# A hybrid layer stack on one core: the second bias's products spread over eight steps, and unread products at two waits

## The chip, the cores and the metric

The kernel runs on one core of one Trainium2 chip. The metric is device time in microseconds (us) of one execution, lower is better. TensorE is the matrix engine (PE in the profile, PEld its weight loads), VectorE is DVE, ScalarE is ACT, GpSimd is POOL; SyncE (SP) issues all DMAs.

## The reference

Four blocks are applied to `x` of 1024 tokens by 256 channels in fp32, each as `x = x + block(layernorm(x))`, but for the expert block, whose own residual adds its normalized input as well:

```python
x = x + attn_a(layernorm(x))     # state space layer, 32 heads of 64, states of 128
x = x + ffn(layernorm(x))        # experts
x = x + attn_b(layernorm(x))     # state space layer, 64 heads of 8, one group of states of 128
x = x + ffn(layernorm(x))        # experts, the same weights

def ffn(x):
    aff = sigmoid(x @ wa)                      # 16 routed experts
    topk_p, topk_i = top_k(aff, 2)             # two of them for each token
    combine = one_hot(topk_i) * (topk_p / sum(topk_p)), summed over the two
    # each expert: (gelu(x @ g + gb) * (x @ w1 + b1)) @ w2 + b2
    routed = sum over e of combine[e] * expert_e(x)
    shared = sum of 2 shared experts
    return x + shared + routed
```

The last bias `b2` of all experts is, for all tokens, one product of the routing weights (16 rows, and two rows of ones for the shared experts) with the 18 rows of `b2`.

## The kernel before

The engines' programs are written out by hand, one after the other in the order in which each engine is to work; the engines are tied by semaphores alone. `Waits.wait_ge` leaves out a wait that its engine has already passed. Each block is a stage: `first_layer`, `experts(0)`, `second_layer`, `experts(1)`.

**Experts.** There are 18 experts (the two shared ones first), each for two halves of 512 tokens: 36 steps. `up(s)` (L899) makes the two up products of a step in one of two wide PSUM tiles (`wide_of(turn)`, two banks each): two calls of `product` (L682), each six matmuls of 128x512, since an fp32 factor is held as a high and a low part and three of the four part products are made for each of two blocks of channels. ScalarE takes the gelu of the first bank, GpSimd multiplies it by the token's routing weight (`bcast`, a row that a DMA spreads over the partitions), VectorE (L1842) multiplies it into the second bank, which gives the hidden values (`hid`), and splits them in two parts (L1853, L1855). `down(s)` (L917) multiplies these by the expert's down weights: four chunks of tokens by three part products, twelve matmuls of 128x256, which add up in the four upper banks (`out_cols(c)`) over all experts. On TensorE the up products of step s are followed by the down products of step s - 2. Up products need the hidden values of two turns before, since they overwrite their tile.

**Routing weights.** VectorE finds them between the first steps (`route_first`, `route_second`). TensorE turns them with one transpose (L938) into the tile of turn 4, behind `down(1)` and ahead of `down(2)`. VectorE, after it has split the hidden values of step 2, copies them out (`route_third`, L1906); SyncE stores them to `scratch_e` and loads from there the rows for the gates and `combT`, the left operand for the bias. `up(5)` (turn 6) writes the tile again and waits for that copy. GpSimd's residual addition (L2349) stands at step 8.

**Second bias.** At step `BIAS_AT` = 8, between `up(8)` and `down(6)`, TensorE makes eight fp32 products (L946), one for each chunk of 128 tokens: 18 partitions by 128 on the left, 18 by 256 on the right. Such an fp32 product is two records in the trace.

**Second layer.** The heads are done in 16 quads of four. `exponents(k)` (L992) makes four products of 128x512, each into one of the four upper banks (`open_bank` waits until the unit four places before has been read). ScalarE takes their exponentials, VectorE and GpSimd mask them (L2004, L2421). Between them stand the products that add to the states (L1007) and read them (L1015), which VectorE works off, and `inside(k)` (L1034), which adds the masked products up in a wide tile. The fourth exponent of quad 1 takes the bank that the second addition to the states had, and waits until VectorE has read that.

**Unread products.** `keep_busy(bank, n)` (L662) makes n fp32 products of `ones` by `ones`, 128x128, into the first columns of a bank; each is overwritten later and read by nobody. The kernel has 75 of them, 150 records, mostly at the layer norms.

Of the kernel before, what the change touches and what calls it, by code (L numbers as in the profile page):

```python
# [13 lines left out]
P = 128  # L14
T, D = 1024, 256
NC = T // P
# [3 lines left out]
BANK = 512  # L20

HA, PA = 32, 64
PAIRS = HA * PA // P
# [5 lines left out]
XT = WB // P  # L29
# [11 lines left out]
TILE_OF_B = [2 + 2 * i if kind == "z" else i if i < 2 else 2 * i - 1 for kind, i in SEQ_B]  # L41

GATE_AT, SQUARE_AT, ADD_AT = (9, 11, 13), (8, 11, 13), (12, 14)
N_CONST = 17

ROWS_OF_SUMS = (0, 32)
# [2 lines left out]
EXPERTS = E + SH  # L49
# [154 lines left out]
def narrow_units(n):  # L204
    return [("nar0", n), ("nar1", n), ("narT", n)]
# [94 lines left out]
def n_router(n, name):  # L300
    return len(ROUTER) * n + ROUTER.index(name) + 1
# [6 lines left out]
STEPS = [(ORDER[p], half) for p, half in PLACES]  # L308
STEP_OF = {place: s for s, place in enumerate(PLACES)}

COMB_TURN = 4
BIAS_AT = 8
# [6 lines left out]
def turn_of(s):  # L319
    return s if s < COMB_TURN else s + 1  # L320
# [15 lines left out]
def hybrid_block(nc, io):  # L336
    with ExitStack() as ctx:
# [3 lines left out]
        sem = Sems(nc, ctx, SEMS)  # L341
# [25 lines left out]
        wide = [psum[:, 2 * i * BANK:(2 * i + 2) * BANK] for i in range(2)]  # L367
# [9 lines left out]
        def lay_out(**sizes):  # L377
            at, out = 0, {}
            for name, n in sizes.items():
                out[name] = arena[:, at:at + n]  # L380
                at += n
            assert at <= ARENA, at
            return out
# [28 lines left out]
        def term_of(j, i):  # L412
# [4 lines left out]
        G_ = lay_out(w=SLOTS * (2 * KD * F + D), wa=KD * E, gb=EXPERTS, ub=EXPERTS, aff=NC * E, key=NC * E, one=NC * E,  # L417
                     comb=NC * E, c2=NC * E, m1=NC, m2=NC, km=NC, den=NC, combT=T, b2=D, gate=3 * BANK, hid=2 * BANK)
# [58 lines left out]
        def bank_of(unit):  # L477
            n = N_FILLED[unit] - 1
            at = 4 + (n if n < AGAIN else n - AGAIN) % 4
            return psum[:, at * BANK:(at + 1) * BANK]  # L480

        def wide_of(turn):
            return wide[turn % 2]


        def sync_program(sp):
# [109 lines left out]
            def second_layer():  # L596
# [14 lines left out]

                on.wait_ge(sem["bconst"], N_CONST)
                on.wait_ge(sem["down"], len(STEPS))
# [28 lines left out]
        def tensor_program(pe):  # L642
            on = Waits(pe)

            def open_bank(unit):

                n = N_FILLED[unit] - 1
                if n >= 4:
                    before = FILLED[n - 4]
                    if before in N_DVE:  # L650
                        on.wait_ge(sem["dve_done"], N_DVE[before])
                    else:
                        on.wait_ge(sem["act_done"], N_ACT[before])
                return bank_of(unit)
# [7 lines left out]
            def keep_busy(bank, n):  # L662

                on.wait_ge(sem["const"], 1)
                for _ in range(n):
                    pe.matmul(bank[:, 0:P], ones[:, :], ones[:, :], start=True, stop=True)

            def layer_norm(k, q):

                bank = open_bank(("ln", k, q))  # L670
                if k == 2:
                    on.wait_ge(sem["x_out"], (1, 2, 4, 4)[q])
                keep_busy(bank, BUSY_NORM[k][q])
                for c in (2 * q, 2 * q + 1):
                    on.wait_ge(sem["ln_v"], NC * k + c + 1)
                    on.wait_ge(sem["ident"], 16)
                    for i in range(KD):
                        at = (c % 2) * KD + i
                        m = pe.transpose(bank[:, at * P:(at + 1) * P], v[:, c, i * P:(i + 1) * P], ident[:, :])
                m.then_inc(sem["unit"], 1)  # L680

            def product(bank, t, half, k):  # L682

                on.wait_ge(sem["split"], t + 1)
                on.wait_ge(sem["dve_done"], N_DVE["ln", k, 2 * half + 1])
                for n, (q, (i, j)) in enumerate((q, p) for q in range(KD) for p in PRODUCTS):
                    m = pe.matmul(bank, split[:, t % SPLITS, i, q, :], vT[:, j, q, half * BANK:(half + 1) * BANK],  # L687
                                  start=(n == 0), stop=(n == 3 * KD - 1))
                m.then_inc(sem["proj"], 1)
# [206 lines left out]
            def experts(n):  # L896
                k, first = 2 * n + 1, TILE_E[n]

                def up(s):  # L899
                    i, half = STEPS[s]  # L900
                    p, turn = PLACES[s][0], turn_of(s)
                    if turn - 2 == COMB_TURN:
                        on.wait_ge(sem["router"], n_router(n, "combT"))
                    elif turn >= 2:
                        on.wait_ge(sem["hid"], len(STEPS) * n + turn - 2 - (turn - 2 > COMB_TURN) + 1)
                    elif n == 0:
                        on.wait_ge(sem["x_s"], 2 * turn + 2)
                    else:
                        on.wait_ge(sem["y_out"], 2 * XT)
                        on.wait_ge(sem["rms"], 1)  # L910
                    for part in range(2):
                        product(wide_of(turn)[:, part * BANK:(part + 1) * BANK], first + 2 * p + part, half, k)

                def out_cols(c):
                    return psum[:, 4 * BANK + c * D:4 * BANK + (c + 1) * D]

                def down(s):  # L917
                    p, half = PLACES[s]
                    on.wait_ge(sem["hid_lo"], len(STEPS) * n + s + 1)
                    on.wait_ge(sem["down_lo"], EXPERTS * n + p + 1)  # L920
                    on.wait_ge(sem["act_done"], N_ACT["narT", n])
                    on.wait_ge(sem["dve_done"], N_DVE["ln", k, 3])
                    for c in range(4 * half, 4 * half + 4):
                        for m_, (iw, ih) in enumerate(PRODUCTS):
                            m = pe.matmul(out_cols(c), split_hid[:, s % 2, ih, (c % 4) * P:(c % 4 + 1) * P],  # L925
                                          split_down[:, p % DOWNS, iw], start=(p == 0 and c % 2 == 0 and m_ == 0),
                                          stop=(p == EXPERTS - 1 and m_ == 2), skip_group_check=True)
                    m.then_inc(sem["down"], 1)

                head(E, k, narrow_units(n), 2 * n + 1, lambda: up(0))  # L930
                up(1)
                up(2)
                down(0)
                up(3)
                down(1)
                on.wait_ge(sem["router"], n_router(n, "comb"))
                on.wait_ge(sem["hid"], len(STEPS) * n + COMB_TURN - 1)
                pe.transpose(wide_of(COMB_TURN)[:, 0:P], G_["comb"], ident[:, :]).then_inc(sem["exp_step"], 1)  # L938
                down(COMB_TURN - 2)
                for s in range(COMB_TURN, len(STEPS)):  # L940
                    up(s)
                    if s == BIAS_AT:
                        on.wait_ge(sem["comb"], 16 * (n + 1))
                        on.wait_ge(sem["b2"], 16 * (n + 1))
                        for c in range(NC):
                            pe.matmul(out_cols(c), G_["combT"][0:EXPERTS, c * P:(c + 1) * P], G_["b2"][0:EXPERTS, :],  # L946
                                      start=False, stop=False, skip_group_check=True)
                    if s != COMB_TURN and not (n == 0 and s == len(STEPS) - 1):
                        down(s - 2)
                    if n == 0 and s == len(STEPS) - 2:  # L950
                        down(s - 1)
                down(len(STEPS) - 2)
                if n == 0:
                    layer_norm(2, 0)
                    keep_busy(wide_of(turn_of(len(STEPS) - 2)), BUSY_LAST)
                down(len(STEPS) - 1)

            def second_layer():
# [11 lines left out]
                def turned_sums(name, src):  # L970

                    bank = open_bank(name)
                    on.wait_ge(sem["bconst"], N_CONST)
                    for q in range(HB * NC // P):
# [17 lines left out]
                def exponents(k):  # L992

                    b = k % 3
                    on.wait_ge(sem[f"mv{b}"], 64 * (k // 3 + 1))
                    for j in range(4):
                        bank = open_bank(("D", 4 * k + j))
                        pe.matmul(bank, steady[:, b, j], moving[b][:, j], start=True, stop=True).then_inc(sem["unit"], 1)  # L998

# [131 lines left out]

            first_layer()
            experts(0)
            second_layer()
            experts(1)


# [979 lines left out]
        def gpsimd_program(pool):  # L2117
# [235 lines left out]
            def fixed(part):  # L2353
# [30 lines left out]
                else:  # L2384
# [3 lines left out]
                    for row in ROWS_OF_SUMS:  # L2388
                        for piece in range(2):
                            select(st3, ALU.not_equal, 1.0, -(row + 2 * piece), [[-1, 2], [0, SUB]], 1)  # L2390
                assert done[0] == (5, 11, N_CONST)[part]

# [147 lines left out]
```

## Time and profile before

| | |
|---|---|
| timed runs | 1095.44, 1095.44, 1093.54 us; median 1095.44 |
| the profiled execution's own time | 1095.1 us |
| its span, from the first to the last instruction | 1093.8 us |
| mean granted clock of TensorE | 0.983 of full speed |
| busy: TensorE, VectorE, GpSimd, ScalarE | 95%, 71%, 63%, 56% of the span |
| first expert stage | about 570 to 752 us |
| second layer | about 752 to 915 us |
| second expert stage | about 915 to 1094 us |

Times in the trace are microseconds from the span's start. A matmul's record includes the tail until its result is there, which overlaps the next one; for the pace the starts are compared. The granted clock (PEclk) is 1.00 for 2.4 GHz and 0.50 for 1.2 GHz. What stands in square brackets behind a row is how long the engine sat idle ahead of it and who ended that.

### The profile page before, as it was taken

Reading aid. Unit: us, or ns where it says so; the run is one execution under the profiler, and the core shown is the slowest. Engines: PE = TensorE matmul, PEld = TensorE weight load, DVE = VectorE, ACT = ScalarE, POOL = GpSimd, SP = SyncE. Lnnn points to the kernel's source line nnn. Section 1 sums busy time; section 2 is a strip of 40 time slices with the busy share of each in tenths; the row PEclk is TensorE's granted clock in tenths of the full one; section 3 lists DMA queues with packets and bytes.
Section 4 is the critical chain, followed back from the end, with each engine's and each line's share of the span. In section 5 each row is a group of like instructions: output and inputs, shape, how many; then the busy total and the mean of one; then the engine's idle time right before and its main releaser. Section 6 shows DMA issues by size and latency. Waiting matters only on the chain.

```text
span 1093.8 us, 23878 instructions
## 1 busy us (share of the span) xinstructions
PE 1043.8 (95%) x9902; PEld 863.2 (79%) x9902; DVE 781.0 (71%) x1186; ACT 612.7 (56%) x945; POOL 690.1 (63%) x684
## 2 busy tenths in 40 slices
PE   8899999999999999999998999998888899999998
PEld 6688888888888888888887888887653577788887
DVE  5789887888878889788867346555858765745554
ACT  5887877776867777786715223224853534322221
POOL 4977786787867788686772667644366242356553
PEclk9999999999999999999999899999999999999999
DMA  3322211211112212101020643303111120323311
GB/s 110 111 69 78 68 59 49 69 50 68 59 49 68 73 46 78 47 24 49 1 70 5 229 135 102 103 18 107 49 53 22 35 65 3 132 95 113 123 55 39
DMA packets 47217, 75.96 MB, mean 69 GB/s; under 512 B 11330, under 2 KB 34150, under 8 KB 47110
## 3 DMA queue, kind: packets, MB, share of 16 engines
q1 hardware_dynamic: 47110, 74.44, 21.3%
q8 instruction: 79, 1.29, 0.5%
q14 instruction: 28, 0.23, 0.1%
HBM read 68.13 MB, written 2.36 MB: 64 GB/s over the span
## 4 chain that ended last, share of the span: by engine, by line
PE 66%; DVE 21%; POOL 6%; ACT 3%; issue 3%; DMA 1%; DVEq 0%; SPq 0%; POOLq 0%
PE psum L687 35%; PE psum L925 9%; DVE arena L1690 7%; PE psum L659 4%; PE psum L775 4%; PE psum L767 3%; PE psum L820 3%; DVE arena L1727 2%; PE psum L1034 2%; DVE arena L1952 1%; PE psum L998 1%; PE psum L1068 1%; DVE v L1987 1%; DVE arena L1746 1%; DVE arena L1754 1%
## 5 line engine op out<-in xcount | busy, mean ns | idle before, releaser
L687 PE MATMUL psum<-vT,split 128*128 128x512 f32 x2136 | 542.3, 404 | 10.3 <-DVE arena L1690 5.5
L687 PEld LDWEIGHTS psum<-vT,split 128*128 128x128 f32 x2136 | 394.0, 191 | 100.6 <-DVE arena L1690 7.0
L1690 DVE SCALAR_TENSOR_TENSOR arena<-psum,arena 128x1023 f32<-128x1023 f32 (+2 forms) x208 | 265.7, 1277 | 76.1 <-ACT arena L1226 52.9
L2138 POOL TENSOR_TENSOR split<-arena,split 128x256 fp32r<-128x256 f32 x178 | 132.9, 759 | 63.1 <-ACT split L1151 62.8
L2345 POOL TENSOR_TENSOR arena<-arena,bcast 128x512 f32<-128x512 f32 x64 | 83.3, 1303 | 117.7 <-ACT arena L1398 101.2
L1398 ACT ACTIVATE arena<-psum,arena 128x512 f32<-128x512 f32 x72 | 49.7, 690 | 180.7 <-PE psum L687 180.6
L1226 ACT ACTIVATE arena<-psum,arena 128x512 f32<-128x512 f32 x160 | 109.3, 691 | 72.0 <-PE psum L687 71.0
L1842 DVE SCALAR_TENSOR_TENSOR arena<-psum,arena 128x512 f32<-128x512 f32 x72 | 53.9, 748 | 122.6 <-POOL arena L2345 117.6
L925 PEld LDWEIGHTS psum<-split_down,split_hid 128*128 128x128 f32 x864 | 115.8, 196 | 10.5 <-DVE split_hid L1855 3.6
L925 PE MATMUL psum<-split_down,split_hid 128*128 128x256 f32 x864 | 118.8, 289 | 2.8 <-DVE split_hid L1855 2.8
L2165 POOL TENSOR_TENSOR arena<-arena,v 128x1021 f32<-128x1021 f32 x32 | 76.4, 2388 | 43.1 <-DVE arena L1690 43.1
L1243 ACT ACTIVATE arena<-arena 128x1024 f32<-128x1024 f32 x80 | 84.3, 1059 | 31.4 <-POOL arena L2165 19.8
L659 PE MATMUL psum<-ident,arena 128*128 128x128 f32 x568 | 73.0, 274 | 8.3 <-POOL arena L2195 4.8
L659 PEld LDWEIGHTS psum<-ident,arena 128*128 128x128 f32 x568 | 64.1, 141 | 20.0 <-POOL arena L2195 8.5
L1151 ACT CAST split<-arena 128x256 fp32r<-128x256 f32 x178 | 67.2, 401 | 4.4 <-DMA arena<-in_wd 4.4
L1855 DVE TENSOR_TENSOR split_hid<-arena,split_hid 128x512 fp32r<-128x512 f32 x72 | 64.8, 900 | 2.5
L767 PEld LDWEIGHTS psum<-arena 128*128 128x128 f32 x512 | 61.2, 192 | 2.0
L767 PE MATMUL psum<-arena 128*128 128x128 f32 x512 | 62.5, 275 | 0.0
L775 PE MATMUL psum<-arena 128*64 128x64 f32 x1792 | 61.2, 223 | 0.7 <-POOL arena L2173 0.7
L775 PEld LDWEIGHTS psum<-arena 128*64 128x64 f32 x1792 | 56.3, 138 | 6.3 <-issue 5.1
L2156 POOL TENSOR_TENSOR bcast<-bcast,arena 128x1024 f32<-128x1024 f32 x32 | 60.9, 1902 | 0.0
L1853 DVE CAST split_hid<-arena 128x512 fp32r<-128x512 f32 x72 | 41.5, 576 | 17.5 <-PE psum L925 10.5
(223 smaller groups left out, 1516.3 us busy)
## 6 DMA issues: line engine op xcount, KB each, us to landing
bcast<-scratch_a SPq DMA_DIRECT2D x32, 512.0 KB, 3.7
bcast<-scratch_e SPq DMA_DIRECT2D x32, 512.0 KB, 4.2
arena<-in_w_a SPq DMA_DIRECT2D x16, 768.0 KB, 4.4
arena<-in_wg SPq DMA_DIRECT2D x36, 128.0 KB, 3.6
arena<-in_wu SPq DMA_DIRECT2D x36, 128.0 KB, 3.5
arena<-in_wd SPq DMA_DIRECT2D x36, 128.0 KB, 3.9
arena<-in_wout_a SPq DMA_DIRECT2D x8, 256.0 KB, 2.7
arena<-in_w_b SPq DMA_DIRECT2D x10, 128.0 KB, 4.9
```

Of the source, the lines that this page charges most:

```text
L659: m = pe.transpose(bank[:, i * P:(i + 1) * P], src, ident[:, :])
L687: m = pe.matmul(bank, split[:, t % SPLITS, i, q, :], vT[:, j, q, half * BANK:(half + 1) * BANK], start=(n == 0), stop=(n == 3 * KD - 1))
L767: m = pe.matmul(chunk(bank, i), chunk(cv_a[:, j % 2, 1 + g, :], c), chunk(cv_a[:, j % 2, 3 + g, :], c), start=True, stop=True)
L775: m = pe.matmul(out[half, :], lhs[:, half], rhs, start=True, stop=True)
L925: m = pe.matmul(out_cols(c), split_hid[:, s % 2, ih, (c % 4) * P:(c % 4 + 1) * P], split_down[:, p % DOWNS, iw], start=(p == 0 and c % 2 = ...
L1151: act.copy(split[:, t % SPLITS, 0], raw).then_inc(sem["hi"], 1)
L1226: act.activation(tile[:, hs], wide_of(t)[:, hs], ACT.Identity, scale=w[:, TAPS - 1:TAPS], bias=0.0).then_inc(sem["tap0"], 1)
L1243: act.activation(tile, tile, ACT.Silu).then_inc(sem["silu"], 1)
L1690: dve.scalar_tensor_tensor(out=tile[:, s:T], in0=bank[:, 0:T - s], scalar=cw_a[:, j, i, TAPS - 1 - s:TAPS - s], in1=tile[:, s:T], op0=ALU. ...
L2138: pool.tensor_tensor(split[:, t % SPLITS, 1], raw, split[:, t % SPLITS, 0].bitcast(F32), ALU.subtract).then_inc(sem["split"], 1)
L2165: pool.tensor_tensor(tile, tile, term_of(j, i)[:, far:T], ALU.add).then_inc(sem["light"], 1)
L2345: pool.tensor_tensor(gate, gate, row_buf[b][:, half * BANK:(half + 1) * BANK], ALU.mult).then_inc(sem["gated"], 1)
```

## The change

The eight bias products are no longer made together at step 8, but one a step, at steps 8 to 15, each at the same place between `up(s)` and `down(s - 2)`. At the routing weights six unread products stand ahead of the transpose and nine behind it, ahead of `down(2)`; the wait for the hidden values, which the transpose had, now stands ahead of the six. In the second layer twelve unread products stand ahead of the fourth exponent of quad 1, in the second wide tile, which nobody uses yet.

```diff
+BUSY_COMB, BUSY_QUAD = (6, 9), 12
...
                 down(1)
+                on.wait_ge(sem["hid"], len(STEPS) * n + COMB_TURN - 1)
+                keep_busy(wide_of(COMB_TURN), BUSY_COMB[0])
                 on.wait_ge(sem["router"], n_router(n, "comb"))
-                on.wait_ge(sem["hid"], len(STEPS) * n + COMB_TURN - 1)
                 pe.transpose(wide_of(COMB_TURN)[:, 0:P], G_["comb"], ident[:, :]).then_inc(sem["exp_step"], 1)
+                keep_busy(wide_of(COMB_TURN)[:, BANK:2 * BANK], BUSY_COMB[1])
                 down(COMB_TURN - 2)
                 for s in range(COMB_TURN, len(STEPS)):
                     up(s)
-                    if s == BIAS_AT:
+                    if BIAS_AT <= s < BIAS_AT + NC:
+                        c = s - BIAS_AT
                         on.wait_ge(sem["comb"], 16 * (n + 1))
                         on.wait_ge(sem["b2"], 16 * (n + 1))
-                        for c in range(NC):
-                            pe.matmul(out_cols(c), G_["combT"][0:EXPERTS, c * P:(c + 1) * P], G_["b2"][0:EXPERTS, :],
-                                      start=False, stop=False, skip_group_check=True)
+                        pe.matmul(out_cols(c), G_["combT"][0:EXPERTS, c * P:(c + 1) * P], G_["b2"][0:EXPERTS, :],
+                                  start=False, stop=False, skip_group_check=True)
...
                     for j in range(4):
+                        if (k, j) == (1, 3):
+                            on.wait_ge(sem["z"], PAIRS + XT)
+                            keep_busy(wide[1], BUSY_QUAD)
                         bank = open_bank(("D", 4 * k + j))
```

## Rows read from the trace of the kernel before

**Rows 1.** The page: its span, and the engines' busy time.

```profile
span 1093.8 us, 23878 instructions
PE 1043.8 (95%) x9902; PEld 863.2 (79%) x9902; DVE 781.0 (71%) x1186; ACT 612.7 (56%) x945; POOL 690.1 (63%) x684
```

**Rows 2.** Stretches of both expert stages: length, each engine's busy time, PEclk, DMA.

```profile
600.35:603.70 3.35, 3.35 (x13) 2.96 (x13) 1.15 (x3) 0.00 (x0) 0.00 (x0) 0.50 0.09 24
...
621.40:624.20 2.80, 2.80 (x14) 2.43 (x14) 0.75 (x1) 0.00 (x0) 2.80 (x2) 0.99 1.07 367
624.20:631.10 6.90, 6.90 (x24) 5.53 (x23) 1.63 (x5) 0.00 (x0) 2.69 (x1) 0.51 0.41 137
...
632.50:650.00 17.50, 17.50 (x102) 15.31 (x101) 8.20 (x12) 4.82 (x11) 11.85 (x16) 1.00 0.51 158
...
968.95:972.35 3.40, 3.40 (x15) 3.28 (x15) 0.41 (x1) 0.00 (x0) 1.60 (x1) 0.50 0.00 0
```

**Rows 3.** TensorE's timeline in the first expert stage: start, length, line, operands, count.

```profile
598.04 0.30 PE L938 MATMUL psum<-ident,arena 128*128 128x128 f32 x1 [0.77 <-DVE arena L1842]
599.57 2.37 PE L925 MATMUL psum<-split_down,split_hid 128*128 128x256 f32 x12 [1.23 <-DVE split_hid L1855]
...
608.23 1.60 PE L925 MATMUL psum<-split_down,split_hid 128*128 128x256 f32 x12
609.91 2.63 PEld L687 LDWEIGHTS psum<-vT,split 128*128 128x128 f32 x12 [0.29 <-DVE arena L1842]
...
621.39 4.50 PE L946 MATMUL psum<-arena 18*128 18x256 f32 x16
...
632.47 1.60 PE L925 MATMUL psum<-split_down,split_hid 128*128 128x256 f32 x12
633.91 2.96 PE L687 MATMUL psum<-vT,split 128*128 128x512 f32 x12
636.71 1.60 PE L925 MATMUL psum<-split_down,split_hid 128*128 128x256 f32 x12
```

**Rows 4.** TensorE's timeline in the second expert stage.

```profile
942.32 0.30 PE L938 MATMUL psum<-ident,arena 128*128 128x128 f32 x1 [0.78 <-DVE arena L1842]
943.85 2.00 PE L925 MATMUL psum<-split_down,split_hid 128*128 128x256 f32 x12 [1.22 <-DVE split_hid L1855]
...
952.52 1.59 PE L925 MATMUL psum<-split_down,split_hid 128*128 128x256 f32 x12
...
965.33 3.72 PE L946 MATMUL psum<-arena 18*128 18x256 f32 x16
968.97 2.93 PE L925 MATMUL psum<-split_down,split_hid 128*128 128x256 f32 x12
...
974.78 1.60 PE L925 MATMUL psum<-split_down,split_hid 128*128 128x256 f32 x12
```

**Rows 5.** The other engines' timeline at the routing weights, first expert stage.

```profile
598.83 0.69 DVE L1855 TENSOR_TENSOR split_hid<-arena,split_hid 128x512 fp32r<-128x512 f32 x1
599.43 0.28 DVE L1906 COPY arena<-psum 128x128 f32<-128x128 f32 x1
...
607.70 2.55 POOL L2345 TENSOR_TENSOR arena<-arena,bcast 128x512 f32<-128x512 f32 x2 [9.20 <-DMA bcast<-scratch_e]
```

**Rows 6.** TensorE's timeline: five unread products, ahead of the last layer norm.

```profile
915.35 1.28 PE L666 MATMUL psum<-ones 128*128 128x128 f32 x10
```

**Rows 7.** The timeline at the second quad's exponents.

```profile
813.95 2.59 DVE L2004 TENSOR_TENSOR bcast<-bcast,arena 128x512 f32<-128x512 f32 x2
...
814.09 0.50 PE L998 MATMUL psum<-split_gate,split_down 128*128 128x512 f32 x1 [1.61 <-DVE v L1990]
814.52 1.33 PE L1007 MATMUL psum<-arena 64*128 64x512 f32 x4
```

**Rows 8.** The stretch behind them, columns as in rows 2.

```profile
815.30:818.40 3.10, 3.10 (x57) 1.01 (x58) 3.07 (x3) 0.00 (x0) 3.10 (x3) 0.50 0.23 42
```

## The prediction

> **What bounds the kernel now.** I read the totals first, then the granted clock stretch by stretch, then TensorE's order of work around the three places that the change touches. The profiled execution took 1095.1 us, 1.3 us more than its span; TensorE is busy for 95% of it [rows 1]. In both expert stages it works without a pause from the first routed steps on: a step is twelve up products and twelve down products, 1.44 us from the start of the down products to that of the next up products (632.47 to 633.91) and 2.80 us for the up products (633.91 to 636.71), 4.24 us together [rows 3]. So in these stages the time is the number of columns divided by the granted clock. The reader should look at the column PEclk: it stands at 1.00 (2.4 GHz) nearly everywhere, and at 0.50 (1.2 GHz) in a few stretches. One follows the waits at the routing weights, from 600.35 to 603.70: TensorE had done one transpose between two waits of 0.77 and 1.23 us [rows 2, 3]; the second stage has its like. Others begin while the eight bias products run (624.20 to 631.10) [rows 2] or at their end (968.95 to 972.35) [rows 2]. There TensorE had been busy all the time, but with operands of 18 partitions. The change goes for these stretches and for a third kind, in the heads of the second layer (815.30 to 818.40) [rows 8].
>
> **Part 1, the bias products one a step.** None is added or removed. Eight products are sixteen records; in the second stage they take from 965.33 to 968.97, 3.64 us, so 0.455 us a product [rows 4], almost all at full clock. Then come the down products (1.44) and the up products (2.80) [rows 3]. At full clock the bundle, the down and the up behind it would last 3.64 + 1.44 + 2.80 = 7.88 us. They lasted 632.47 - 621.39 = 11.08 us in the first stage [rows 3] and 974.78 - 965.33 = 9.45 us in the second [rows 4]. The half clock cost 3.20 and 1.57 us. With one product among twenty-four full ones a step becomes 4.24 + 0.455 = 4.70 us with a tenth of it on 18 partitions. I take it that the clock stays at 2.4 GHz, as it does through the plain steps from 632.50 on [rows 2]: gain 3.20 + 1.57 = 4.77 us. The bounds: nothing regained (0) and all (4.77). The change of operand between the full and the 18-partition products, which was met once a stage, now comes eight times; no row shows its price apart, I take 0, and at most 0.1 us a product, about half of the 0.2275 us of a record [rows 4], 16 x 0.1 = 1.6 us. What the pause hid: GpSimd's long residual addition stands at the same step and is not on TensorE's path, because a step's gate is needed only two steps later.
>
> At this place the trace and a rule part. In the stretch 621.40 to 624.20 TensorE is busy for 2.80 of 2.80 us, and the clock falls right behind it [rows 2]. The Trainium skill, "TensorE: Matmul & The Clock Gate", section "What's actually happening", says that the gate follows how busy the engine has been recently. By that rule an engine that never paused should have kept its clock, the bundle would not be the cause, and spreading it would give nothing (the first rival); by the rows it is the only thing in either stage that comes just ahead of a fall without a wait.
>
> **Part 2, fifteen unread products at the routing weights, in each stage.** An unread product is two records; ten records last 1.28 us with the last one's tail of 0.27 us, so 0.112 us a record and 0.225 a product [rows 6]. Six cost 1.35 us, nine 2.02 us. The wait for the hidden values (597.9, where the transpose at 598.04 was let go [rows 3]) now comes ahead of the six, and the transpose behind them: 598.04 + 1.35 = 599.39. It ends 0.30 us later at 599.69. VectorE, who copies it, was free at 599.43 anyway, since it was at its splitting of the hidden values until then [rows 5]; so the copy comes 0.26 us later, not 1.35. Behind the copy on the path: the store of the weights, the row's load, GpSimd's gate at 607.70, which waited for that load [rows 5], VectorE's hidden values, and the up products at 609.91, which waited for those [rows 3].
> TensorE itself: nine unread products from 599.46 to 601.48, the down products to 602.92, and the two ups to 602.92 + 5.60 = 608.52 at full clock. Before, the down products began at 599.57 and the two ups ended at 608.23 [rows 3]. So the fill is paid with 1.91 us and gets the half clock back, and is 0.29 us behind. Its next down products end at 608.52 + 1.44 = 609.96, which is ahead of the released ups at 609.91 + 0.26 = 610.17. First stage: +0.26 us, set by the row's path; that the half clock is gone buys nothing there.
> Second stage: the transpose stood at 942.32, so it comes at 943.67, the nine end at 945.76, the down products at 947.20, the two ups at 952.80; before it was 952.52 [rows 4]. +0.28 us. Bounds: if no half clock is regained, the down products are late by 1.91 and 945.76 - 943.85 = 1.91 us, of which the first stage hides 0.24 us (609.91 against 608.23 + 1.44): +1.67 and +1.91. At the other end, a fill that delays nothing and regains all: 0 in the first stage, which waits for the row anyway, and -(8.67 - 7.04) = -1.63 in the second (943.85 to 952.52 against 1.44 + 5.60) [rows 4]; six and nine products between two waits that leave 1.23 us of room [rows 3] can't do that, so I stay by the sum.
>
> **Part 3, twelve unread products before the fourth exponent of the second quad.** 12 x 0.225 = 2.69 us. The fourth exponent came at 814.09 after a wait of 1.61 us [rows 7], so the third ended at 812.48, and what follows it could have begun a tail of 0.27 us earlier, at 812.2. The fourth then comes about 812.2 + 2.69 = 814.9, 0.8 us later than before. The state additions behind it come at about 815.3 in place of 814.52; they lasted 1.33 us with the clock falling under them [rows 7], and at full clock end by about 816.4. VectorE reads them after its masks, which last from 813.95 to 816.54 [rows 7]: just in time. The half clock from 815.30 to 818.40 would go, which spares TensorE up to 1.55 us, but VectorE has no gap in that stretch (3.07 of 3.10 us busy) [rows 8] and TensorE waits for it afterwards. I take 0, since it is VectorE whose row is full. Bounds: -1.55 (all of it arrives) and +0.8 (the delay arrives).
>
> **Sum.** -4.77 + 0.26 + 0.28 + 0 = -4.23 us on 1095.1: 1090.9. The three timed runs were 1095.44 twice and 1093.54, so the profiled execution is within 0.4 us of their median; forecast 1091.0.
>
> **Rivals.**
> 1. The bundle isn't what lowers the clock, and it falls in these steps as before (the rule above). Then parts 2 and 3 alone remain: 1095.1 + 0.54 = 1095.6. Against: it fell in both stages at the same instructions, and in none of the plain steps. Chance 0.05.
> 2. Slower: the unread products are work on TensorE's path and buy no clock, since the wait of 0.8 us ahead of them stays and the falls come from it. Price 1.67 + 1.91 + 0.8 = 4.4 us, at down products and exponents. It decides the sign once the bias gives back less than 4.4 us; slower by 0.2% (2.2 us) needs the bias to give less than 2.2: to 1099.5. For it: waits as short as this stand close before a fall. Against: the two waits of 0.77 and 1.23 us [rows 3] become one. Chance 0.05.
> 3. The falls don't lie the same in each execution, since one and the same bundle cost 3.20 us in one stage and 1.57 in the other. Then the bias gives back 1.57 twice: 1095.1 - 3.14 + 0.54 = 1092.5. If besides a fill of part 2 regains nothing in the second stage, because nothing had fallen there, 1.63 us more: 1094.1. For it: the timed runs lie 1.9 us apart, about one such stretch. Chance 0.20, half of it below 1093.2.
> 4. Part 3 bears fruit: the states go round faster once TensorE is at full clock, and a later fall is put off as well: 1.5 to 3 us more, 1088 to 1089.5. Against: VectorE is full there. Chance 0.15.
>
> **How the numbers follow.** Forecast 1091.0, own range 1089.7 to 1092.5, chance 0.55. A measurement tells about 0.2% from no change, here 2.2 us: faster is below 1093.2. Faster: 0.55 + 0.15 + 0.10 = 0.80. Within: 0.05 + 0.10 = 0.15. Slower: 0.05. The range goes to 1088.6 and 1093.8; it leaves out rivals 1 and 2, the upper end of 3 and the lower of 4, together under 0.2.
>
> **What the profile after would show.** Right: the unread products rise from 150 records by 2 x 30 + 24 to 234; PEclk 1.00 through steps 8 to 15 of both stages, each 4.70 us; 1.00 behind the transpose, with down products about 1.9 us later and the second up ending 0.3 us later than before; the second quad's fourth exponent about 0.8 us later and VectorE's order unmoved. Wrong: a half clock within the steps that hold a bias product (part 1), one behind the nine unread products (part 2), gaps of VectorE around 816 (part 3), or steps with a bias product longer than 4.8 us at full clock (the change of operand has a price).

## The result, and the profile after

The changed kernel takes 1102.72 us (median of nine runs, 1097.37 to 1106.06) against 1095.3 us of the kernel before (nine runs, 1093.52 to 1097.79): a ratio of 1.0064, with an interval of 1.0044 to 1.0084. The forecast was 1091.0 with a range of 1088.6 to 1093.8, faster with a chance of 0.8. It was slower, by about 7 us. The profiled execution after took 1103.7 us, its span is 1102.4 us. The page after, lines that answer to [rows 1]:

```profile
span 1102.4 us, 24043 instructions
PE 1052.5 (95%) x9986; PEld 866.3 (79%) x9986; DVE 785.1 (71%) x1186; ACT 613.1 (56%) x945; POOL 695.0 (63%) x684
```

The stretches of the expert stages after (length, each engine's busy time, PEclk, DMA), which answer to [rows 2]:

```profile
600.00:618.00 18.00, 18.00 (x108) 15.80 (x108) 9.36 (x13) 4.48 (x9) 8.10 (x8) 1.00 0.63 206
618.00:660.00 42.00, 42.00 (x219) 32.56 (x218) 23.82 (x29) 9.95 (x21) 32.63 (x35) 1.00 0.49 161
962.00:1010.00 48.00, 48.00 (x253) 37.78 (x252) 26.21 (x32) 11.55 (x25) 30.81 (x27) 1.00 0.35 114
```

All half clocks of the expert stages are gone from this execution: 1.00 behind the routing weights and through the steps with a bias product, as forecast. So the clock does what was forecast, and the kernel is slower. Where the time went is seen by comparing the starts of the same work in the two traces:

| the same place | before | after | after minus before |
|---|---|---|---|
| first down products, first expert stage | 591.43 | 591.30 | -0.13 |
| ups released by the first row | 609.91 | 609.85 | -0.06 |
| turning the narrow product, second layer | 762.17 | 761.35 | -0.82 |
| first exponent of quad 0 | 807.94 | 808.82 | +0.88 |
| the 128 small products ahead of the first `finish` | 862.27 | 860.77 | -1.50 |
| the first of the 24 products of the output | 895.07 | 900.43 | +5.36 |
| turning the narrow product, second expert stage | 929.40 | 936.56 | +7.16 |
| down products of step 3, second expert stage | 952.52 | 959.99 | +7.47 |
| last 36 down products | 1085.03 | 1093.64 | +8.61 |

The first expert stage gained 0.7 us, the second lost about 1.4, and the heads of the second layer, between 862 and 930, lost over 8 us. TensorE's timeline in the first expert stage after, which answers to [rows 3]:

```profile
597.82 1.60 PE L668 MATMUL psum<-ones 128*128 128x128 f32 x12 [0.68 <-DVE arena L1849]
599.26 0.27 PE L941 MATMUL psum<-ident,arena 128*128 128x128 f32 x1
599.37 2.17 PE L668 MATMUL psum<-ones 128*128 128x128 f32 x18
601.30 1.67 PE L927 MATMUL psum<-split_down,split_hid 128*128 128x256 f32 x12
602.80 5.76 PE L689 MATMUL psum<-vT,split 128*128 128x512 f32 x24
608.41 1.60 PE L927 MATMUL psum<-split_down,split_hid 128*128 128x256 f32 x12
609.85 2.96 PE L689 MATMUL psum<-vT,split 128*128 128x512 f32 x12
...
618.33 2.96 PE L689 MATMUL psum<-vT,split 128*128 128x512 f32 x12
621.22 0.69 PE L950 MATMUL psum<-arena 18*128 18x256 f32 x2
621.84 1.69 PE L927 MATMUL psum<-split_down,split_hid 128*128 128x256 f32 x12
623.37 2.96 PE L689 MATMUL psum<-vT,split 128*128 128x512 f32 x12
```

The fill at the routing weights went as worked out: the two ups end at 608.41, 0.31 us later than before once the start of the stage (-0.13) is taken off (forecast 0.29). But a step with one bias product lasts 623.37 - 618.33 = 5.04 us, not 4.70. Its weight loads show why (the same stretch on PEld, the engine's weight loads):

```profile
621.22 0.29 PEld L950 LDWEIGHTS psum<-arena 18*128 18x128 f32 x2 [0.36 <-issue]
621.84 1.49 PEld L927 LDWEIGHTS psum<-split_down,split_hid 128*128 128x128 f32 x12 [0.33 <-issue]
623.25 2.64 PEld L689 LDWEIGHTS psum<-vT,split 128*128 128x128 f32 x12
```

Elsewhere a load starts ahead of the product that uses it (623.25 for the ups at 623.37). At the bias product it starts together with it, and so does the load behind it: the loads stand idle for 0.36 and 0.33 us at each change of kind. The kernel before has the same two waits at its bundle, once a stage (second expert stage, PEld):

```profile
965.33 3.31 PEld L946 LDWEIGHTS psum<-arena 18*128 18x128 f32 x16 [0.36 <-issue]
968.97 2.64 PEld L925 LDWEIGHTS psum<-split_down,split_hid 128*128 128x128 f32 x12 [0.33 <-issue]
```

That one kind is plain fp32 and the other the split operands is not enough for it. The unread products are plain fp32 too, on 128 partitions, and the loads of the down products behind them start without a wait, at 601.27 against 601.30 for the first product:

```profile
601.27 1.49 PEld L927 LDWEIGHTS psum<-split_down,split_hid 128*128 128x128 f32 x12
```

What the bias products have beside that is operands of 18 partitions; no run varied that number.

In the heads the reader is to look at the waits put down to "issue", time in which TensorE waited for nothing that the profile shows. TensorE's timeline after, the three long ones:

```profile
862.18 0.66 PE L1053 MATMUL psum<-ident,arena 64*128 64x64 f32 x8
864.33 1.44 PE L1053 MATMUL psum<-ident,arena 64*128 64x64 f32 x22 [1.48 <-issue]
...
867.36 1.19 PE L1041 MATMUL psum<-v,arena 64*32 64x64 f32 x101 [0.45 <-DVE arena L2018]
871.24 0.67 PE L1041 MATMUL psum<-v,arena 64*32 64x64 f32 x27 [2.69 <-issue]
...
900.29 0.21 PE L1041 MATMUL psum<-v,arena 64*32 64x64 f32 x1 [2.53 <-issue]
900.43 7.13 PE L1075 MATMUL psum<-arena 128*128 128x256 f32 x24
```

They stand in the middle of a group of equal instructions, once with a single record of 128 left to do. In the kernel before, the thirty records of the first group (L1046 there) and the 128 of the second (L1034) go through unbroken:

```profile
863.68 2.00 PE L1046 MATMUL psum<-ident,arena 64*128 64x64 f32 x30
...
867.27 1.47 PE L1034 MATMUL psum<-v,arena 64*32 64x64 f32 x128 [0.47 <-DVE arena L2011]
```

At the second and the third of the long waits the clock falls to half (stretches as above):

```profile
871.00:877.00 6.00, 5.76 (x162) 4.38 (x162) 2.22 (x3) 2.65 (x6) 0.00 (x0) 0.50 0.12 27
897.80:900.20 2.40, 0.00 (x0) 0.00 (x0) 0.20 (x1) 0.00 (x0) 2.40 (x2) 1.00 0.03 7
901.50:905.00 3.50, 3.50 (x10) 2.81 (x9) 0.00 (x0) 0.00 (x0) 2.79 (x5) 0.55 0.02 5
```

The kernel before had such waits too, nine of them in this layer, but none above 1.29 us. I counted the matmul records from the first transpose of the tokens on (804.08 before, 804.95 after) to each such wait. Before, they stand at 584, 710, 837, 963, 1343, 1471, 1598, 1725 and 2361: 126 to 128 apart, or a multiple. With a weight load for each record that is some 254 instructions. After, they stand at 1188, 1315 and 2205. Their sum is not what differs: 7.0 us before, 6.7 after. A theory follows: TensorE's instructions arrive in blocks, a block's end comes at a fixed count of instructions, and what a stall costs depends on where in the work that end falls. Parts 2 and 3 add instructions and move it. The Trainium skill, "Runtime: NRT & Kernel Launch", section "Instruction fetch mechanics", says that an engine's instructions are refilled in blocks of 256, and that crossing a block's end is mostly hidden. The distance agrees with the trace; "mostly hidden" doesn't hold for this layer, with 7.0 us of such waits before. That these waits are waits for instructions is inferred from their even distances, not seen in the profile.

### The profile page after: what moved, and what is told of

Read it like the earlier page. It is cut to its first block, busy times and chain, and to the rows that moved or that the text cites. A ratio compares the mean times of both kernels' runs of the same rounds, so it can differ in the third digit from the quotient of the medians.

```text
span 1102.4 us, 24043 instructions
## 1 busy us (share of the span) xinstructions
PE 1052.5 (95%) x9986; PEld 866.3 (79%) x9986; DVE 785.1 (71%) x1186; ACT 613.1 (56%) x945; POOL 695.0 (63%) x684
## 3 DMA queue, kind: packets, MB, share of 16 engines
q8 instruction: 79, 1.29, 0.5%
## 4 chain that ended last, share of the span: by engine, by line
PE 66%; DVE 23%; POOL 4%; issue 3%; ACT 3%; DMA 0%; DVEq 0%; POOLq 0%
PE psum L689 35%; PE psum L927 9%; DVE arena L1697 7%; PE psum L661 4%; PE psum L777 4%; PE psum L769 4%; PE psum L822 3%; DVE arena L1734 2%; DVE v L1994 1%; DVE arena L1959 1%; DVE arena L1753 1%; DVE arena L1761 1%; PE psum L950 1%; PE psum L1041 1%; DVE v L1997 1%
## 5 line engine op out<-in xcount | busy, mean ns | idle before, releaser
L689 PEld LDWEIGHTS psum<-vT,split 128*128 128x128 f32 x2136 | 389.5, 188 | 99.4 <-DVE arena L1697 7.2
L927 PEld LDWEIGHTS psum<-split_down,split_hid 128*128 128x128 f32 x864 | 111.4, 191 | 10.7 <-issue 5.3
L1860 DVE CAST split_hid<-arena 128x512 fp32r<-128x512 f32 x72 | 46.7, 649 | 14.0 <-PE psum L927 7.9
```

## The experiments

Two theories were to be told apart: that the loss is the direct price of the added and spread products, or that it comes from the place of the instruction stream's stalls. All experiments were timed in five rounds, each row of runs beside its own runs of the kernel before.

**Part 1 alone (bias_only).** The bias products one a step, and no unread products:

```diff
+BIAS_PER, BIAS_STEPS = 1, [8, 9, 10, 11, 12, 13, 14, 15]
...
-                    if s == BIAS_AT:
+                    if s in BIAS_STEPS:
+                        at = BIAS_STEPS.index(s) * BIAS_PER
...
-                        for c in range(NC):
+                        for c in range(at, at + BIAS_PER):
```

> Only part 1: the eight bias products one a step, no unread products added. Theory (each lone bias product makes its step 0.80 us longer at full clock, since the weights of the two kinds of product don't load ahead of each other): steps 8 to 15 last 5.05 us each, 6.4 us in all against 6.84 and 5.21 us that the bundles cost before, so -0.4 us in the first stage, +1.2 us in the second, +0.8 us in all: about 1096. Rival (the loss of the changed kernel comes from the unread products alone): the gain forecast for part 1 shows, steps of 4.70 us, 1090.5.

Measured: 1096.72 against 1093.19 us, ratio 1.0028 (1.0011 to 1.0044). Slower, and by more than the +0.8 us expected. The stalls in the heads stand at the same nine counts as before (584 to 2361), as they must, since nothing was added. Its steps 8 to 15 are at PEclk 1.00:

```profile
618.00:660.00 42.00, 42.00 (x219) 32.56 (x218) 24.10 (x29) 10.26 (x23) 33.57 (x36) 1.00 0.51 173
```

So the lone products' price is real, and the clock held. That the sum is worse than +0.8 is taken up under the table.

**Part 2 alone (comb_only).** The six and nine unread products in both stages, as in the diff of the change.

> Only part 2: six and nine unread products at the routing weights of both stages. By the direct cost +0.1 us in the first and +0.3 us in the second stage: 1095.8. If the longer instruction stream in front of the second layer is what rearranges TensorE's stalls for instructions in the heads (the stalls that the profile calls issue), this kernel, which has as many instructions ahead of the heads as the changed one, shows stalls of over 2 us there, and 1099 to 1102. If the loss in the second layer comes from part 3: no such stalls, 1095.8.

Measured: 1093.89 against 1093.19 us, ratio 1.0001 (0.9984 to 1.0018). The stalls did move: one of 2.54 us at count 1315 (before: 1343) and one of 0.25, in place of nine. But their sum fell from 7.0 to 2.8 us, and the time stayed the same. So moving them can be harmless, even to one wait as long as the changed kernel's; the expectation of 1099 was wrong. The long one stands three records ahead of the end of its group:

```profile
866.17 1.44 PE L1037 MATMUL psum<-v,arena 64*32 64x64 f32 x125 [0.46 <-DVE arena L2014]
870.15 0.42 PE L1037 MATMUL psum<-v,arena 64*32 64x64 f32 x3 [2.54 <-issue]
```

**Part 3 alone (quad_only).** The twelve unread products in the second quad.

> Only part 3: twelve unread products ahead of the fourth exponent of quad 1. Theory that this is what harms the second layer: stalls of over 2 us behind quad 8 as in the changed kernel, 1099 to 1102. Theory that the instructions ahead of the second layer matter: about 1095 here, the half clock behind the exponent gone, VectorE's order unmoved.

Measured: 1092.51 against 1093.19 us, ratio 0.999 (0.9969 to 1.001). One stall of 1.56 and one of 0.24 us. No loss from it by itself that is clear of the noise.

**Waits that have passed (pad_30).** The kernel before with instructions added that do nothing:

```diff
+                    if n == 0 and 18 <= s < 28:
+                        for _ in range(3):
+                            pe.wait_ge(sem["const"], 1)
```

> The kernel before with thirty waits that have long been passed, three in each of ten steps of the first expert stage, on TensorE: no product more, only 30 instructions more, which is what fifteen unread products (a weight load and a product each) put in front of the second layer. If the place of the instructions in the stream decides the stalls in the heads: stalls rearranged as in the changed kernel, 1098 to 1101. If it doesn't: 1095.4, the same as before within 0.2%.

Measured: 1091.84 against 1093.19 us, ratio 0.9981 (0.9964 to 0.9999). The padded steps mostly last 4.24 us as ever, so the waits are free; the stalls moved by only about 7 records and stayed of the old kind (eight, of at most 1.57 us). It doesn't tell the theories apart, but it gives a tool: a way to move the stalls without a product. It is a caution as well: its interval ends just under 1 though nothing but passed waits was added, so a ratio of 0.998 by itself is no proof that an edit gains anything.

**The changed kernel again (after_again), and parts 2 and 3 together (comb_quad).**

> The changed kernel once more, beside the others of this row. Part 1 alone came to 1.0028 of before, part 2 to 1.0001, part 3 to 0.999, together 1.0019, but the changed kernel to 1.0064. If the parts add up and the difference is the spread of the executions: 1.002, 1095. If parts 2 and 3 together rearrange the stalls for instructions in the heads (3 stalls of 1.5 to 2.7 us instead of 9 of at most 1.3): 1.005 to 1.007 again, with the three stalls in the same places.

Measured: 1099.64 against 1094.89 us, ratio 1.0044 (1.0026 to 1.0061), with stalls at the same counts as in the first profile, 1188, 1315 and 2205, and one at 1442. The two measurements of the same kernel, 1.0064 and 1.0044, agree within their intervals.

> Parts 2 and 3 without part 1 (the bias products together again): if the two rearrange the stalls together, about 1.003 to 1.004 of before with three long stalls in the heads as in the changed kernel; if the parts add up: 0.999 to 1.000.

Measured: 1097.88 against 1094.89 us, ratio 1.0028 (1.0009 to 1.0048). Neither part costs anything alone that shows, and together they cost 3 us. Its timeline has the same breaks as the changed kernel's, 8 and 22 records, 101 and 27, 127 and 1, and one more of 1.55 us at 1442:

```profile
863.54 0.66 PE L1053 MATMUL psum<-ident,arena 64*128 64x64 f32 x8
865.83 2.60 PE L1053 MATMUL psum<-ident,arena 64*128 64x64 f32 x22 [1.63 <-issue]
...
870.36 1.73 PE L1041 MATMUL psum<-v,arena 64*32 64x64 f32 x101
873.62 0.44 PE L1041 MATMUL psum<-v,arena 64*32 64x64 f32 x27 [1.54 <-issue]
...
902.62 0.21 PE L1041 MATMUL psum<-v,arena 64*32 64x64 f32 x1 [1.98 <-issue]
```

**Moving the stalls there, and back (pad_230, comb_quad_pad).** The first adds 230 passed waits to the kernel before (23 in place of 3 in the diff of pad_30), the second adds 420 (21 a step in steps 14 to 33) to parts 2 and 3.

> The kernel before with 230 waits that have long been passed, 23 in each of ten steps of the first expert stage; nothing else. Thirty such waits cost no time in their steps and moved TensorE's stalls for instructions 7 matmul records ahead, so 230 should move them by 53 or 54, which is where parts 2 and 3 together put them (1343 before, 1188 and 1315 with 24 records of part 3 in the count, 127 apart). If the place of the stalls is the cause: long stalls within L1046's thirty records, within the 128 records behind them and ahead of L1068's twenty-four, and 1.002 to 1.004 of before. If it is something else in the unread products (their place at the waits, the heads' banks): 1.000.

Measured: 1098.38 against 1095.59 us, ratio 1.0022 (1.0005 to 1.004), with stalls at 1160, 1287, 1414, 2049 and 2177. The first two of them in TensorE's timeline:

```profile
861.28 0.44 PE L1049 MATMUL psum<-ident,arena 64*128 64x64 f32 x4
863.44 1.87 PE L1049 MATMUL psum<-ident,arena 64*128 64x64 f32 x26 [1.73 <-issue]
...
867.25 1.50 PE L1037 MATMUL psum<-v,arena 64*32 64x64 f32 x97
870.48 0.46 PE L1037 MATMUL psum<-v,arena 64*32 64x64 f32 x31 [1.74 <-issue]
```

No product was added, and the stalls are within four records of where parts 2 and 3 put them (the 24 records of part 3 taken off), with a loss of the same size. The page explains the quarter of a record for each wait: it counts 15 more instructions in pad_30 and 115 more in this kernel (23993 against 23878), one for each two waits. At two instructions a record that is 7.5 and 57.5 records, and the stalls moved by 7 and 56.

> Parts 2 and 3, and 420 passed waits in twenty steps of the first expert stage, which should move the stalls another 98 records, by 127 with part 2's own 29, one whole distance between two stalls, so that in the heads they stand where part 3 alone has them (one of 1.56 us). If the place of the stalls is the cause: 0.999 to 1.000 of before instead of 1.0028. If not: 1.0028 again.

Measured: 1094.15 against 1095.59 us, ratio 0.9994 (0.9974 to 1.0015): the loss of 1.0028 is gone though still more instructions were added. The page counts 210 more instructions than comb_quad's, 105 records, and the stalls moved by 104. The thirty records of L1056 (L1053 in comb_quad) go through unbroken and the block's end falls four records ahead of the end of the next group:

```profile
861.44 2.00 PE L1056 MATMUL psum<-ident,arena 64*128 64x64 f32 x30
...
865.02 1.44 PE L1044 MATMUL psum<-v,arena 64*32 64x64 f32 x124
868.48 0.30 PE L1044 MATMUL psum<-v,arena 64*32 64x64 f32 x4 [2.02 <-issue]
```

That is, but for one record, where part 2 alone had its long wait, and it is as harmless here as there. Part 3 alone has its own seven records further on.

**The changed kernel with the same 420 waits (after_pad).**

> The changed kernel (all three parts) with the 420 passed waits that brought parts 2 and 3 from 1.0028 back to 0.9994. If the changed kernel's loss is the lone bias products (1.0028) and the place of the stalls (about 1.003) and nothing else: the second goes, 1.002 to 1.003 of before, and the stalls in the heads stand where parts 2 and 3 with the waits had them. If something further in the sum of the parts is at work: 1.004 or more.

Measured: 1095.86 against 1093.12 us, ratio 1.0024 (1.0007 to 1.0042), stalls at 1339, 1466 and 2101. What is left is the size of part 1 alone.

The loss lies where the theory puts it. From the first exponent of quad 0 to the first down products of the second expert stage the profiled executions of the four kernels with stalls at the bad places took 134.1 us (after, 808.82 to 942.87), 132.8 (after_again), 135.9 (comb_quad) and 133.8 (pad_230). The kernel before took 127.8 (807.94 to 935.71), comb_only 128.2, quad_only 126.2, comb_quad_pad 127.1, after_pad 127.9, and none of the other five more than 130.0. These are single executions, and comb_quad's was the slowest of its twelve, so the size of the loss is the 3 us of the medians and not this difference.

**Bias products by twos and by fours (bias_2x4, bias_4x2).** The edit of bias_only with `BIAS_PER, BIAS_STEPS = 2, [8, 9, 10, 11]` for bias_2x4 and `4, [8, 9]` for bias_4x2.

> Part 1 with two bias products a step, at steps 8 to 11, no unread products. Theory (0.455 us a product and 0.35 us for each change between the two kinds and back): a step is 4.24 + 0.91 + 0.35 = 5.50 us, four of them 5.0 us over plain steps against 6.4 of one a step and 3.64 + 0.35 of the bundle at full clock: 1.4 us a stage less than one a step, 2.8 us in all, so 1.0002 of before. Rival (the price hangs on each product, not on the change): 2 x 0.80 a step, 6.4 us a stage as before, 1.0028.

Measured: 1093.34 against 1094.89 us, ratio 0.9979 (0.9964 to 0.9995). A step with two products lasts 5.49 us (620.21 to 625.70), as the theory had it; the total came out lower than its 1.0002.

> Part 1 with four bias products a step, at steps 8 and 9, no unread products. By the change of kind: 2 x (1.82 + 0.35) = 4.3 us a stage over plain steps if the clock holds, 2.1 us a stage less than one a step: 1095.3 - 1.2 = 0.999 of before. If 1.8 us of 18-partition products at one place are enough to lower the clock, a half clock stands behind them in some executions, 1.6 us more each: 1.001.

Measured: 1092.6 against 1094.89 us, ratio 0.9982 (0.9964 to 0.9999). A step with four lasts 6.34 us, and no half clock follows. TensorE's timeline:

```profile
618.29 2.96 PE L688 MATMUL psum<-vT,split 128*128 128x512 f32 x12
621.19 1.99 PE L948 MATMUL psum<-arena 18*128 18x256 f32 x8
623.11 1.69 PE L926 MATMUL psum<-split_down,split_hid 128*128 128x256 f32 x12
624.63 2.96 PE L688 MATMUL psum<-vT,split 128*128 128x512 f32 x12
```

Steps of 5.04, 5.49 and 6.34 us with one, two and four products: 0.45 and 0.425 us for each further product, and 5.04 - 4.24 - 0.45 = 0.35 us for the change to the other kind and back. The price hangs on the change, not on the product. So fewer and larger bundles that the clock still bears are better than lone products (0.998 against 1.0028). That they are better than the whole bundle is less sure: pad_30 came to 0.9981 too.

**By fours, and part 3 (bias_4x2_quad).**

> Four bias products a step at steps 8 and 9 (0.9982 alone) and part 3 (0.999 alone), without part 2. If the parts add up where nothing else moves the stalls: 0.997, about 1091.5, with the one or two stalls in the heads that part 3 alone had. Rival: part 3's 0.999 was no effect, 0.998.

Measured: 1091.14 against 1095.59 us (six runs), ratio 0.9953 (0.9934 to 0.9971). It is faster than the kernel before and the changed one, and by more than the sum of its parts; the stalls are two, of 1.84 and 0.52 us. Whether the surplus is more than the spread of the runs I can't say.

**All runs in one table.** Each run lists its mean granted clock beside its span. The mean over the runs of span x (1 - clock) is about what half clocks took, and span x clock what would be left without them:

| kernel | runs | mean span | taken by half clocks | the rest | ratio |
|---|---|---|---|---|---|
| before, beside the first four | 35 | 1092.5 | 14.3 | 1078.1 | |
| before, beside the next four | 34 | 1093.6 | 15.5 | 1078.0 | |
| before, beside the three after those | 23 | 1093.7 | 16.1 | 1077.7 | |
| before, beside after_pad | 17 | 1092.5 | 14.3 | 1078.2 | |
| changed kernel, first measurement | 9 | 1100.9 | 11.4 | 1089.5 | 1.0064 |
| after_again | 11 | 1098.6 | 8.6 | 1090.0 | 1.0044 |
| bias_only | 12 | 1095.3 | 12.0 | 1083.4 | 1.0028 |
| bias_2x4 | 12 | 1091.9 | 10.0 | 1081.9 | 0.9979 |
| bias_4x2 | 12 | 1091.6 | 11.4 | 1080.2 | 0.9982 |
| comb_only | 12 | 1092.6 | 14.7 | 1077.9 | 1.0001 |
| quad_only | 12 | 1091.3 | 11.5 | 1079.8 | 0.999 |
| pad_30 | 12 | 1091.2 | 13.3 | 1077.9 | 0.9981 |
| comb_quad | 12 | 1096.4 | 13.6 | 1082.8 | 1.0028 |
| comb_quad_pad | 12 | 1093.1 | 13.8 | 1079.3 | 0.9994 |
| pad_230 | 12 | 1096.7 | 18.3 | 1078.5 | 1.0022 |
| bias_4x2_quad | 6 | 1090.3 | 10.4 | 1079.9 | 0.9953 |
| after_pad | 12 | 1095.2 | 9.6 | 1085.6 | 1.0024 |

From the spread of the runs a difference of half clocks is uncertain by about 2 us either way in this table, by 3 in some rows, and one of the rest by 1 to 2. Two things are to be seen. In bias_only part 1 saves 14.3 - 12.0 = 2.3 us of half clock and adds 1083.4 - 1078.1 = 5.3 us of work; by twos it saves 5.5 and adds 3.9, by fours 4.1 and 2.2. And the loss of the badly placed stalls shows as waiting in comb_quad (the rest 4.8 us up). In pad_230 it looks more like half clock (18.3 in place of 16.1 in its own runs of before), but that is within the uncertainty.

## Why the prediction was wrong, point by point

**Part 1, the clock: right in kind.** Counting the profiled executions, a half clock began in or right behind the bundle in 11 of the 14 stages of the seven kernels that kept it whole, and in none of the 14 stages of the seven that split it. The three without one are the second stages of quad_only and pad_230 and the first of pad_30. The rule that a busy engine keeps its clock, rival 1, is refuted for these products: TensorE was busy all through the bundle, and splitting it into eight, four or two pieces kept 2.4 GHz. Plain fp32 by itself isn't the reason, since the fill of unread fp32 products on 128 partitions ran at PEclk 1.00 (600.00 to 618.00).

**Part 1, the change of operand: the term that failed.** I wrote that no row showed its price, took 0, and bounded it by 0.1 us. The sign that I had named for it, steps longer than 4.8 us at full clock, is what came: 5.04. It is 0.35 us for each lone product, 16 x 0.35 = 5.6 us for the change, less the 0.7 us that two bundles pay anyway: +4.9 us in the sum where I had 0, which takes back all of the 4.77 us. The step that failed is the bound: I halved the pace of a record and looked at the products alone, where the weight loads stand idle at the change, 0.36 us ahead of a bias product and 0.33 behind it. The nearest rows were there: in the kernel before the loads have the same waits put down to issue, 0.36 us ahead of each bundle, and behind it 0.33 us in the second stage and 0.65 in the first, where the clock had fallen.

**Part 1, the gain: right in size as far as the runs tell, but read from one execution.** The half clocks that splitting removes come to 2.3 us over the runs of bias_only, 5.5 by twos and 4.1 by fours, and in the 14 profiled stages with a whole bundle to 1.7 us a stage, 3.4 an execution. So 4.77 us is at the upper end. Rival 3 (the falls don't lie the same in each execution) had this right in kind: three of the 14 stages had no fall at all. For bias_only itself: gain 2.3, price 5.3, +3.0 us, which is the ratio of 1.0028.

**Part 2: right in size, partly by luck.** +0.07 us at the released ups (forecast +0.26), the second up of the first stage ends at +0.31 (forecast +0.29). But the forecast for the released ups was "set by the row's path", and that path was not late: GpSimd's gate came at 606.59, 1.1 us earlier than before (607.70), instead of 0.26 later.

```profile
606.59 2.67 POOL L2352 TENSOR_TENSOR arena<-arena,bcast 128x512 f32<-128x512 f32 x2 [8.21 <-DMA bcast<-scratch_e]
```

The released ups then followed the down products at once (608.41 and 609.85, the plain 1.44 us), so TensorE's own order set them. Why the row came earlier wasn't tried. Nor is there a half clock to regain each time: it follows these waits in 8 of the 16 profiled stages without the fill, and in none of the 12 with it. Alone part 2 is 1.0001; what it regains is paid for by its own 1.9 us.

**Part 3: right where it stands.** From the third exponents' group to the fourth exponent it takes 815.79 - 812.00 = 3.79 us after and 2.96 before, 0.83 us more (forecast 0.8), and VectorE's next state begins at 817.38, 5.38 us behind that group against 5.34 before. Alone it is 0.999, which its interval doesn't tell from 1.

**What was not in the prediction at all.** I costed parts 2 and 3 where they stand and took the rest of the program as it was. Together they add 54 weight loads and products ahead of and in the heads, and the places where TensorE waits for its instructions move with them, to 8 records into `finish`'s thirty and on from there. That costs 3 us (comb_quad), can be made without a single product (pad_230) and can be taken back by adding still more instructions (comb_quad_pad). With the price of the change the sum becomes -4.77 + 4.9 + 0.26 + 0.28 = +0.7 us; these 3 us on top give +3.7, and +6.1 with the smaller gain of bias_only. Measured were about +7 (1.0064) and +5 (1.0044). Rival 2 (slower, chance 0.05) named the direction but not the reason: the unread products themselves cost almost nothing, and they did keep the clock. The waits put down to issue were in the trace before, nine in the heads and 7.0 us in all, and I passed over them, because nothing in the diff touched them.

**Left open.** Why a block's end that is moved by part 2 alone or by part 3 alone is harmless and both together are not, is known only by where the end falls: 8 records (4 in pad_230) into `finish`'s thirty, against 3 or 4 records ahead of the end of the next group. Which of the stalls in a bad place makes the loss wasn't tried, nor what decides the length of a stall: their sum doesn't tell (7.0 us before, 6.7 after, 2.8 in comb_only, which takes as long as before). The differences are 3 us of 1095, with intervals of about 2 us either way, so it is the two tests in opposite directions, and the length of the heads, that carry this reading, and not one ratio.

## What to carry to other kernels

Before a filler is added to an unrolled stream of many small instructions, look for waits put down to issue and count the records between them: if they come at even distances, each added instruction moves them all, and an edit has to be judged in pairs with a padding of passed waits, which between large products cost no time here. A product of another kind, put between others one at a time, pays for the change each time (0.35 us here): if a bundle lowers the clock, split it no further than the clock asks for. And a gain read from the half clocks of one execution is to be held against the clocks of several runs (here 4.77 us in the one, and 2.3, 5.5 and 4.1 over the runs of three kernels).

## What the runs showed of the hardware that was not expected

- TensorE's weight loads run ahead of the products (0.12 us here, 623.25 against 623.37) but not across a change from the products of the split operands to the fp32 products of 18 partitions, or back: 0.36 and 0.33 us of idle loads each time, 0.35 us on the step. From unread fp32 products of 128 partitions to the split operands they do run ahead (601.27 against 601.30).
- Eight fp32 products of 18 partitions, 3.64 us with TensorE busy throughout, bring a half clock in 11 of 14 cases; four of them (1.92 us to the next down products) in none of the 4 stages that have them.
- TensorE waits for instructions at even distances of 126 to 128 matmul records with a weight load each, for 0.2 to 2.7 us. All those of the expert stages and the second layer stand in the heads, among small products (128 records in 1.48 us). Behind one such wait of 2.69 us 6 us of work went at half clock.
- 230 waits on a semaphore that has long been passed cost no time between large matmuls, and moved those places by 56 records, about a quarter of a record each; the profile counts one instruction for each two of them.
